# A four-layer graph network on one core: its internal tables stored in another row order, and two transfers instead of four for each store of an isolated block

## The reference

```python
edge_index = jnp.stack([src, dst])
x = _layernorm(x + _L0_gnn_ref(x, edge_index, W1, b1, W2, b2), axis=-1)             # GCN after an MLP 64-128-64
x = _layernorm(x + _L1_gnn_ref(x, edge_index, edge_weight, W1, b1, W2, b2), axis=-1) # weighted GCN, 64-128-64
x = _layernorm(x + _L2_gnn_ref(x, src, dst, W, attn_l, attn_r, bias), axis=-1)       # graph attention, softmax per dst
x = _layernorm(x + _L3_gnn_ref(x, src, dst, edge_attr_32, ...), axis=-1)             # message MLP, sum per dst, update MLP
```

## Time and profile before

| | us |
|---|---|
| median of 3 runs | 2941.12 (2938.37 to 2942.83) |
| profiled execution, its own time | 2938.16 |
| its span in the profile | 2936.4 |

### The profile page before, as it was taken

How to read it: one execution, slowest core, us unless ns; L and a number is a source line. 1 busy time by engine, 2 the same in 40 slices (tenths; PEclk the granted TensorE clock), 3 DMA queues, 4 the chain that set the end, 5 groups by cost and what they waited for, 6 DMA issues and landing times.

```text
span 2936.4 us, 39046 instructions
## 1 busy us (share of the span) xinstructions
PE 2171.1 (74%) x10332; PEld 1155.7 (39%) x10332; DVE 1984.6 (68%) x3848; ACT 1429.8 (49%) x2755; POOL 2169.0 (74%) x1666
## 2 busy tenths in 40 slices
PE   3998899968778757777687759998356576666665
PEld 1444444434445324444343434444155233333332
DVE  6665688858888747777599968998699343333332
ACT  2877677745444436665344437777222232223332
POOL 7888878778888268886788858888233688888887
PEclk9999999979898768888789979999555787777777
DMA  7998522224556455555344445555477322222221
GB/s 210 285 271 241 144 57 54 59 58 93 129 130 141 93 128 125 128 133 125 78 112 113 111 95 127 141 137 125 94 191 186 77 62 52 55 57 57 54 53 26
DMA packets 624033, 338.13 MB, mean 115 GB/s; under 512 B 536606, under 2 KB 585100, under 8 KB 623817
## 3 DMA queue, kind: packets, MB, share of 16 engines
q1 hardware_dynamic: 550217, 288.96, 39.1%
q0 software_dynamic: 73600, 46.68, 9.4%
HBM read 203.61 MB, written 130.80 MB: 114 GB/s over the span
## 4 chain that ended last, share of the span: by engine, by line
POOL 57%; issue 19%; PE 9%; DVE 8%; DMA 3%; SPq 1%; ACT 1%; DVEq 0%; POOLq 0%; ACTq 0%
POOL g_row L857 42%; POOL x_with_info L864 8%; POOL out_rows L864 8%; PE bank L1075 2%; PE bank L1098 1%; DVE rT L1685 1%; PE bank L984 1%; PE pair L1055 1%; DMA g_row<-t_x,gidx 1%; PE pair L984 1%; DMA g_row<-in_x,dst_i 1%; DVE x_r L1662 1%; DVE ss L1608 1%; PE pair L1066 0%; DVE w_r L2007 0%
## 5 line engine op out<-in xcount | busy, mean ns | idle before, releaser
L857 POOL DMA_INDIRECT g_row<-t_x,gidx x600 | 808.1, 1347 | 258.6 <-issue 217.3
L1281 ACT ACTIVATE hid<-pair,b_up 128x1000 f32<-128x1000 f32 x375 | 406.0, 1083 | 42.9 <-PE pair L1056 42.1
L1076 PE MATMUL bank<-hid,w_dn 128*64 128x500 f32 x750 | 420.8, 644 | 0.0
L1075 PE MATMUL bank<-hid,w_dn 128*64 128x500 f32 x750 | 420.7, 644 | 0.0
L1055 PE MATMUL pair<-xT,w_top 64*128 64x500 f32 x550 | 316.7, 657 | 15.5 <-ACT hid L1281 15.0
L857 POOL DMA_INDIRECT g_row<-x_with_info,src_i x200 | 275.3, 1377 | 63.8 <-issue 55.8
L1056 PE MATMUL pair<-xT,w_bot 64*128 64x500 f32 x550 | 317.5, 658 | 0.0
L857 POOL DMA_INDIRECT g_row<-t_h,gidx x200 | 261.5, 1307 | 75.7 <-issue 75.7
L857 POOL DMA_INDIRECT g_row<-in_x,dst_i x200 | 261.1, 1306 | 68.7 <-issue 68.1
L1262 ACT ACTIVATE xT<-bank 128x500 f32<-128x500 f32 x275 | 160.2, 583 | 295.3 <-DVE rT L1685 163.2
L864 POOL DMA_INDIRECT out_rows<-n_r,fidx x200 | 248.8, 1244 | 61.6 <-issue 60.3
(11 more groups left out here) (257 smaller groups left out, 5205.0 us busy)
## 6 DMA issues: line engine op xcount, KB each, us to landing
x_in<-in_x_cols SPq DMA_DIRECT2D x100, 250.0 KB
x_with_info<-wide SPq DMA_DIRECT2D x50, 476.0 KB
wide<-in_x SPq DMA_DIRECT2D x50, 448.0 KB
out_rows<-x_r SPq DMA_DIRECT2D x100, 224.0 KB
l_k<-keep_row SPq DMA_DIRECT2D x150, 125.0 KB
l_a<-t_x SPq DMA_DIRECT2D x150, 112.0 KB
l_k<-on_row SPq DMA_DIRECT2D x50, 250.0 KB
t_x<-x_r SPq DMA_DIRECT2D x100, 112.0 KB
```

Source lines behind the costliest of these rows:

```text
L857: return g.indirect_dma_start(out=to, out_offset=None, in_=table, in_offset=bass.IndirectOffsetOnAxis(ap=index[:, tile:tile + 1], axis=0), ...
L1075: T.matmul(run.down[0:D, 0:CH], w_dn[a.stage][:, 0:D], hid[a.b2][:, 0, :], start=True, stop=True)
L1076: T.matmul(run.down[D:128, 0:CH], w_dn[a.stage][:, 0:D], hid[a.b2][:, 1, :], start=True, stop=True)\
L1281: A.activation(hid[a.b2][:, :, :], run.up[a.b2][:, :, 0:CH], ACT.Relu, bias=b_up[:, a.stage:a.stage + 1]).then_inc(Cn["hid"], 1)
```

## The change

It puts the row of partition `p` in chunk order at `p*4 + k` and in block order at `p*8 + j`, so that what a partition stores or loads is one piece of 1 KB or 2 KB. Level A stores a block as two chunks (`chunk_pairs`), two pieces of 1 KB for a partition. The iotas for the gather indices follow, `gbase` with the pair order in it, so that isolated blocks' rows can be stored as they lie: `in_pairs` goes, and each of these stores is two transfers (112 and 13 partitions) and counts 32 instead of 64 on its semaphore. Three loads by chunk go on into every other half row of `l_a` in SBUF (`half(l_a[q])`, levels B, D and M) and stay in pieces of 256 bytes there.

```diff
         def chunks(ap):
-            return ap.rearrange("(c k p) f -> c p k f", k=TC, p=R)
+            return ap.rearrange("(c p k) f -> c p k f", k=TC, p=R)
+
+        def chunk_pairs(ap):
+            return ap.rearrange("(b s p k) f -> b p s (k f)", s=2, k=TC, p=R)
 
         def blocks(ap):
-            return ap.rearrange("(b j p) f -> b p j f", j=TB, p=R)
+            return ap.rearrange("(b p j) f -> b p (j f)", j=TB, p=R)
...
-        def in_pairs(dram_rows, buf):
-
-            to = dram_rows.rearrange("p (s k) f -> p s k f", s=2)
-            frm = buf.rearrange("p (k s f) -> p s k f", s=2, f=D)
-            return [(to[rows, s], frm[rows, s]) for rows in (slice(0, WIDE), slice(WIDE, R)) for s in range(2)]
...
-                        for to, frm in in_two(blocks(base0_d)[a.b], n_view(own_base[a.b % 2][:, :])):
+                        for to, frm in in_two(blocks(base0_d)[a.b], own_base[a.b % 2][:, :]):
...
-                        for to, frm in in_pairs(blocks(t1_d[E:2 * E, :])[a.b], x1_r[a.r4]):
+                        for to, frm in in_two(blocks(t1_d[E:2 * E, :])[a.b], x1_r[a.r4][:, :]):
...
-                        for to, frm in in_pairs(blocks(t2_d[E:2 * E, :])[a.b], h2_r[a.b % 2]):
+                        for to, frm in in_two(blocks(t2_d[E:2 * E, :])[a.b], h2_r[a.b % 2][:, :]):
                             sp.dma_start(to, frm).then_inc(s1_sem[a.b % 2], 16)
                         sp.wait_ge(Cn["rows"], normed(a))
-                        for to, frm in in_pairs(blocks(t3_d[E:2 * E, :])[a.b], x2_r[a.r3]):
+                        for to, frm in in_two(blocks(t3_d[E:2 * E, :])[a.b], x2_r[a.r3][:, :]):
...
-                for to, frm in in_two(blocks(t1_d[0:E, :])[b], n_view(a_rows[b % 2])):
+                for to, frm in in_two(chunk_pairs(t1_d[0:E, :])[b], a_rows[b % 2].rearrange("p (s c) -> p s c", s=2)):
...
-            g.iota(slot_id[:, :], pattern=[[R, NT]], base=1, channel_multiplier=1,
+            g.iota(slot_id[:, :], pattern=[[CH, NC], [1, TC]], base=1, channel_multiplier=TC,
                    allow_small_or_imprecise_dtypes=True).then_inc(s_pool0, 1)
-            g.iota(gbase[:, :], pattern=[[R, NT]], base=E, channel_multiplier=1,
+            g.iota(gbase[:, :], pattern=[[BLK, NI], [1, 2], [2, TC]], base=E, channel_multiplier=TB,
...
-                        at_least(dve, iso_sem1[a.b % 2], 128 * (a.b // 2))
+                        at_least(dve, iso_sem1[a.b % 2], 64 * (a.b // 2))
```

More of the change, by code:

```diff
@@ L664, in ld_a @@
                 at_least(sp, LA["t2"], b - 3)
-                for to, frm in in_two(n_view(a_base[b % 4]), blocks(base0_d)[b]):
+                for to, frm in in_two(a_base[b % 4], blocks(base0_d)[b]):
                     sp.dma_start(to, frm).then_inc(A_ld[b % 4].sem, 16)
@@ L739, in ld_third @@
             def ld_third(b):
-                for to, frm in in_two(n_view(third_in[b % 2]), blocks(t3_d[E:2 * E, :])[b]):
+                for to, frm in in_two(third_in[b % 2], blocks(t3_d[E:2 * E, :])[b]):
                     sp.dma_start(to, frm).then_inc(third_ld[b % 2], 16)
@@ L746, in third @@
                     for b in range(2):
-                        sp.wait_ge(s1_sem[b], 128 * len(range(b, NI, 2)))
+                        sp.wait_ge(s1_sem[b], 64 * len(range(b, NI, 2)))
                         ld_third(b)
@@ L751, in third @@
                         sp.wait_ge(F["rows"], b + 1)
-                        for to, frm in in_two(blocks(t4_d[E:2 * E, :])[b], n_view(third_out[b % 2])):
+                        for to, frm in in_two(blocks(t4_d[E:2 * E, :])[b], third_out[b % 2]):
                             sp.dma_start(to, frm).then_inc(third_st[b % 2], 16)
@@ L928, in _ @@
             for r in range(2):
-                pool.wait_ge([Cn["s0st0"], Cn["s0st1"]][r], 64 * len(range(r, NI, 2)))
+                pool.wait_ge([Cn["s0st0"], Cn["s0st1"]][r], 32 * len(range(r, NI, 2)))
             all_stored(pool, A_st, NI)
@@ L933, in _ @@
             for r in range(2):
-                pool.wait_ge([Cn["s1st0"], Cn["s1st1"]][r], 128 * len(range(r, NI, 2)))
+                pool.wait_ge([Cn["s1st0"], Cn["s1st1"]][r], 64 * len(range(r, NI, 2)))
             all_stored(pool, B_st)
@@ L1609, in first @@
                     if a and a.stage == 0 and a.iso:
-                        at_least(dve, iso_sem0[a.b % 2], 64 * (a.b // 2))
+                        at_least(dve, iso_sem0[a.b % 2], 32 * (a.b // 2))
                         V.tensor_copy(info_r[:, a.b * TB:(a.b + 1) * TB, :], xs_rows[a.b % 4][:, :, D:XW]).then_inc(Cn["info"], 1)
                     if a and a.stage == 1 and a.iso:
-                        at_least(dve, iso_sem1[a.b % 2], 128 * (a.b // 2))
+                        at_least(dve, iso_sem1[a.b % 2], 64 * (a.b // 2))
                         V.tensor_tensor(h2_r[a.b % 2][:, :], run.rows[a.b2][0:R, :], x1_r[a.r4][:, :], ALU.subtract).then_inc(Cn["h2"], 1)
@@ L1653, in rest @@
                                 par, times = iso_stored(a.s - 4)
-                                dve.wait_ge(iso_sem0[par], 64 * times)
+                                dve.wait_ge(iso_sem0[par], 32 * times)
                         if a.stage == 1 and a.s >= 3 and SEQ[a.s - 3].iso:
                             par, times = iso_stored(a.s - 3)
-                            dve.wait_ge(iso_sem1[par], 128 * times)
+                            dve.wait_ge(iso_sem1[par], 64 * times)
                         if a.stage == 2:
@@ L1914, in _ @@
             for r in range(2):
-                dve.wait_ge(iso_sem0[r], 64 * len(range(r, NI, 2)))
-                dve.wait_ge(iso_sem1[r], 128 * len(range(r, NI, 2)))
+                dve.wait_ge(iso_sem0[r], 32 * len(range(r, NI, 2)))
+                dve.wait_ge(iso_sem1[r], 64 * len(range(r, NI, 2)))
             for buf in l_ea:
```

## The result

| | before | changed |
|---|---|---|
| median of 4 runs each, side by side, us | 2940.21 (2938.37 to 2942.83) | 2924.4 (2918.71 to 2926.79) |
| ratio | | 0.9943, 95% interval 0.9926 to 0.996 |
| profiled execution, us | 2938.16 | 2926.79 |
| its span, us | 2936.4 | 2925.0 |

The kernel is faster, by 11.4 us in the two profiled executions, by 15.8 us in the medians and by 0.4 to 0.7% in the ratio; 2931 was forecast. That the number is close says little yet: the forecast is a sum, and the question is whether its terms are where the time went.

A forecast was written before the change was run, and what follows sets the result against it. POOL's gathers and scatters were taken to bound the kernel, leaving some 340 us of 2936 open to change. Terms 6.2 + 3 + 0.5 = 9.7 us, off a median of 2941.1, gave 2931 us, range 2921 to 2943.

The forecast's parts named there:

- More than forecast: Rival: 10 us at level A's end, 4 in level G, 2 at its start, 1.5 at borders: 2924 us; chance 0.16.
- both rings: Waiting cycles: level A's end (`h_r`, next unit, `res`, SP) and level G (loads, product, scan; 6.73 us over two chunks).
- one of its own signs: The prediction was to count as wrong if, among other things, the gathers themselves changed.
- Six issues fewer: Level A's end: six fewer SP issues a round, worth 3.0 to 3.3 us in each of two stalls; 6.2 us taken.
- the last store lands 1.44 us after its issue began: Level A's end: landing time of a round's last store, issued at 1014.31 us, after which DVE's `h_r` starts.
- Reshaped issues: Issues kept in number but given larger pieces: shape doesn't shorten an issue; nothing, 0.05 us either way.
- Level G, 3 us: Level G: larger pieces land `decay_row` up to 0.25 us sooner, step 3.34 to 3.26 us; 3 us taken.
- the closing of the ring: Level G: `decay_row` releases POOL's product, whose end was taken to release the scan; 6.73 us over two chunks.
- The rival in which the product falls on `n_r`: Level G: an earlier POOL product delays DVE's `n_r`, some 18 us, giving 2953; chance 0.12 together with drift.
- Borders, 0.5 us: Before levels C, D, M and G: last stores land slightly sooner, 0 to 1.5 us for four borders; 0.5 taken.
- Table loads and gathers, 0: All levels: gathers from other addresses under 1 us a level either way, taken as 0; unmerged `l_a` loads given nothing.
- Drift: Rival: gather lengths move by DVE's work beside them, either sign, 5 us in the range; shares 0.12 with the slower product.

The follow-up runs named there:

- the half with the isolated blocks alone: Kernel before with only block tables and `gbase` as in the change, two issues per isolated store, chunk tables in the old order: 2939.16 us, ratio 0.9982.

## Why the prediction was right, and where it wasn't

The total was right, 2924.4 us in a range of 2921 to 2943, but a good part of that is luck. It lies at the 2924 of the rival *More than forecast*, whose mechanism, both rings tightening fully, did not happen. Two of the three terms were too large, and what made up for them was not among them. By one of its own signs the prediction is wrong: gathers themselves changed.

*Six issues fewer, 6.2 us.* The place and the mechanism are shown by the waits: `h_r` stalls 4.7 us less (3.9 in the second profiles), and the half with the isolated blocks alone has two stalls of 12.6 us. The step that failed is "the last store lands 1.44 us after its issue began", carried over as it was. It lands after 2.48 and 2.81 us. SP's part of the round fell by more than forecast, 3.9 us in the first round and not 3.1 (L638's four took 2.59 us, L635's two 0.87), and the landing took back 1.0 to 1.4 us a round. The term *Reshaped issues*, nothing, is off too: with the number kept and the pieces larger the round is 0.9 to 1.5 us shorter, and six issues fewer are 2.2 to 2.4 us, under the forecast's 3.0 to 3.3. The medians of 363 and 393 ns that it was read from each mix issues of 112 and 13 partitions, and belong to stores of different sizes. Of the 4.7 us about 2.5 are in level A's end: the first round starts 32.8 us (second profile 34.4) behind the last gather before and 35.2 (36.2) changed. So "POOL's first gather at 1039 to 1040 us" was 1042.67. Where that start is lost has not been tried; level A's units stand further back already soon after the gathers end (the first store of L673 comes 11.7 and 13.2 us behind the last gather before, that of L670 14.5 and 15.1 us changed).

The sentence of the Trainium skill against this term (DMA: Bandwidth & Descriptors, Issuing engines are not separate DMA queues: issuing is usually small beside the transfer) fits the last group, where two issues or four end at nearly the same landing, and not the groups in front of it, whose saved time reached the stalls.

*Level G, 3 us.* Little or nothing came. The step that failed is the closing of the ring: the prediction has the product take "1.23 us, to 2188.79", and the scan end "1.05 us after it", and read this as a release. It is two instructions that run at the same time and get in each other's way; the product is for a later scan. The step ahead of it failed as well: `decay_row` was to land up to 0.25 us sooner, and the product still comes 2.9 to 3.0 us behind its issue. The figure that DVE is busy 95% of the level stood in the prediction as the lower bound, and it was the answer. The rival in which the product falls on `n_r` did not happen.

*Borders, 0.5 us.* POOL's idle time grows by 1.73 us before C and falls by 0.86 us before D, 1.29 before G and 0.17 before M. Two profiles of one kernel differ by up to 0.9, 0.6, 1.6 and 0.1 us there, and by 3.8 before C changed, so the term can't be told from nothing.

*Table loads and gathers, 0.* Wrong, and the largest of all: level M is 8.8 us shorter. "All other gather stages keep their length" held for B, C and D only. The reason given for nothing, that POOL doesn't wait for a landing, is true; but TensorE and DVE do, and where DVE's scan falls sets how long POOL's own instructions last (gathers 1341 ns before, 1302 changed). The prediction had this under *Drift*, by DVE's work beside the gathers and with either sign, but gave it no term. The price of a load into `l_a` was never looked at, as the text said that these loads are not merged; one side of them is. The rows show that this costs SP 0.8 us a chunk, and the experiment with two more issues shows that such a delay is what helps.

*The checks.* 38,896 instructions, as said; 337,482 packets for 339,658; `h_r` 12.0 us for 10; POOL's first gather of level B at 1042.67 us for 1039 to 1040; the level G step 3.32 for 3.28.

## What to carry to other kernels

Before a step is called part of a ring, count: if the producer is two items ahead, the two instructions only share a place in time, and nothing is gained by starting one earlier. At level A's end a cut in the number of issues was worth only the issues ahead of the last group waited for, since those inside it lay under its landing. Where an engine issues gathers back to back, look at what another engine starts just ahead of them: here the timing of a few plain loads moved a scan of DVE by some tenths of a microsecond, and that was worth more than the larger pieces. Try moving such loads by an issue or two before rearranging data.

## What was unexpected of the hardware

- A transfer whose table side is one run of 1 KB and whose SBUF side is in pieces of 256 bytes takes SP longer to issue than one in pieces on both sides: in level M the pair of `l_a` loads took 1.48 us against 0.81.
- Nearly half the packets gone (624,033 to 337,482) lowers the share of SP's queue only from 39.1 to 35.2%, and from 700 to 974 us the same 131 to 132 GB/s take a share of 0.48 instead of 0.60; of the landings waited for, only level A's last store came sooner, after 2.66 us for 2.85. The Trainium skill's rule on transfers below 512 B (DMA: Bandwidth & Descriptors, Specifications) would have made the small stores the dear ones; in the shares there is something of it, in the landings next to nothing.
- A POOL product of 65x500 beside DVE's scan makes the scan 1591 ns on average instead of 1246.
- A gather on POOL that starts inside DVE's scan `x_r<-l_k,x_r,wide` is done 1.08 to 1.11 us behind the scan, up to 2.24 us after its own start; one that starts just ahead of the scan takes its usual 1.27 us.
